# Keys' products moved behind each attention chunk's outputs, with a filled prologue and later weight splits

## The chip, the core and the metric

One NeuronCore of one Trainium2 chip runs the whole program. The metric is the time of one execution on the device, in microseconds (us), from the first to the last instruction with what lies around them; lower is better. TensorE (PE in the rows) multiplies matrices into PSUM banks, VectorE (DVE), ScalarE (ACT) and GpSimd (POOL) work on tiles, SyncE (SP) issues the DMA transfers. Each engine runs its own list of instructions in order, and they wait for one another through semaphores.

## What is computed

A "macaron" block on 4 x 1024 tokens of 128 features: half a gated ternary FFN, a linear attention block with its own small FFN, and half a ternary FFN again (cut to what matters):

```
x = x + 0.5 * ternary_ffn(layernorm(x))
x = x + attention_block(layernorm(x))
x = x + 0.5 * ternary_ffn(layernorm(x))

# ternary_ffn: silu(x@w1*s1) * (x@w2*s2), gelu(h@h1*s), gelu(h@h2*s), h@w3*s
# attention_block:
x = x + linear_attention(ln(x));  x = x + gelu(ln(x) @ Wf1) @ Wf2
# linear_attention, 16 heads of 64, phi = elu + 1:
Q = phi(x @ Wq); K = phi(x @ Wk); V = x @ Wv
S = cumsum(K^T V); z = cumsum(K)           # over tokens
out = (Q S) / max(Q z, 1e-6) @ Wo
```

Products run in a two-part form: each fp32 operand is split into a rounded "high" part and the rest, its "low" part, and two or three matmuls replace one.

## The kernel before

The program has four stages, which follow one another: the first ternary FFN (to about 190 us), the attention (to about 590 us), its small FFN (to about 625 us), the second ternary FFN (to the end). In the ternary FFNs tokens run in tiles of 512, two tiles ("A" and "B") at a time, four pairs per FFN.

**Attention** works in 32 chunks of 128 tokens; two chunks, even `e` and odd `o`, make one pass of `pair(hh)`, and passes 1 to 14 are one loop on TensorE. For chunk `g` TensorE does, in this order: `state_products(g)` (`D`, 64 matmuls of 64 rows by 64 columns, the chunk's K^T V by halves), `scores(g)` (`S`, 64 small ones), the keys' product of the next chunk (`K`, `token_major("K", ...)`: 6 matmuls of 128x512), and `outputs(g)`: first `I`, 64 small matmuls of the queries with the state so far, then `O`, 64 small ones that add the masked scores times the values. After that come the norm's transposes and values (behind an even chunk: also the output projection of the pair before), or the queries and values (behind an odd one), the transposes of keys (`KT`) and of outputs (`OT`), and the next `D`.

VectorE serves each chunk from its own list: `accumulated(g)` adds D's banks to the running state (`sm`, tile `middle`; then `ss`, tile `state`; two halves each), `masked(g)` multiplies the two banks of scores by the mask (`am`), `low_outputs(g)` makes the low parts of the outputs of the chunk before (`ol`), `divided(g)` divides O's banks by the denominator (`ot`), and `phi` finishes keys and queries from ScalarE's exp and relu.

D, I and O write the same four PSUM banks (`OB`, banks 2 to 5). So `outputs(g)` begins with a wait until VectorE has read D's banks, which is the last `ss`; and between I and O stands a wait for the last `am`:

```
emptied([f"O{g}.{j}{m}" for j in range(2) for m in "ab"])        # L962: ahead of I
hold(*([made(X["dve"], f"am{g}b")] if j == 0 else []), ...)      # L976: ahead of O
```

The four other banks (0, 1, 6, 7: `RING`) go round among all 512-column products; `turn()` takes the next one, and a product waits until the reader of the bank's tenant before has done.

**The prologue.** TensorE starts with the transposes of the first two normalised tiles, waits for the first weight split (`weight(0)`: high and low part of piece 0) and does the first products with three matmuls each, until a flag shows that two will do. VectorE makes the high and low parts of the six weight pieces (`high(k)`, `low(k)`: tiles `wh`, `wl`) and, in the first FFN's passes, those of the attention's and the small FFN's weights (`staged(k)`: tiles `fh`, `fl`, `wah`, `wal`, from the transfer into `stage` that SyncE issues). The second tiles' statistics and normalisation (`xn`) come behind `low(1)`, `low(2)`, `high(5)`. In the taken branch TensorE waits for high parts only: pieces 1 and 2 ahead of the hidden layer H1, pieces 3, 4 and 5 ahead of H2. GpSimd makes the low parts of all hidden activations (`al`, L1895).

**The end.** The last two tiles' results are transposed into the same bank 7, so B's transposes wait until VectorE has added A's (`back`, `dve_res`).

Of the kernel before, what the change touches and what calls it, by code (L numbers as in the profile page):

```python
# [5 lines left out]
P = 128  # L6
# [106 lines left out]
def build_kernel(nc, t, out):  # L113
# [37 lines left out]
    with ctx:  # L151
# [223 lines left out]
        def attention_plan():  # L375
# [49 lines left out]
            def transposed(banks, g):  # L425
                for j in range(2):
                    job(banks[j], f"OT{g}.{j}", "dve", f"ol{g}.{j}")
                    act.append(f"oh{g}.{j}")
                    dve.append(f"ol{g}.{j}")
# [25 lines left out]
            for hh in range(NHALF):  # L455
                e, o, last = 2 * hh, 2 * hh + 1, hh + 1 == NHALF
                pairs.append({"pe": len(pe), "act": len(act), "dve": len(dve), "pool": len(pool)})

                for h in range(2):
                    phi(turn(), f"K{o}.{h}")  # L460
                outputs(e)
# [16 lines left out]
                if hh:  # L478
                    job(bank, f"yT{hh - 1}", "dve", f"y{hh - 1}")
                    dve.append(f"y{hh - 1}")  # L480
                transposed((turn(), turn()), e)
                if last:
                    tail(turn(), "N1", "dve_fn", "lo", 1)
                state_products(o, (turn(), turn()))

                if last:
# [8 lines left out]
                    transposed((2, 5), o)  # L495
                    for m in range(2, 4):
# [17 lines left out]
                turn()  # L514
                transposed((turn(), turn()), o)
                state_products(o + 1, (turn(), turn()))
            X = phase(1, pe=pe, act=act, dve=dve, pool=pool)
# [41 lines left out]
        def _(sp):  # L559
# [7 lines left out]
            def tern_dma(f):  # L567
# [8 lines left out]
                for i in range(NI):  # L576
# [4 lines left out]
                    if n == 0:  # L581

                        wait(sp, "dve_wa", "lo", i)
                        sp.dma_start(stage[:, :], t["attn"][i]).then_inc(in_a, 16)
# [5 lines left out]
                    elif n == 0 and i == NI - 2:  # L590

                        wait(sp, "dve_xnA", "xn", off + i + 1)
                        sp.dma_start(ax[:, :, :], view(x1_d)[0]).then_inc(in_ax, 16)
                    for u, U in enumerate(PAIR):
# [85 lines left out]
        def _(pe):  # L680
# [13 lines left out]
            def tern_pe(f, terms, start=None, end=None, head=None):  # L694
# [10 lines left out]
                def back(u, U, n):  # L705

                    wait(pe, f"act_y{U}", "y", n)
                    wait(pe, f"dve_res{before(U, n)[0]}", "res", before(U, n)[1])
                    transposes(ps[7], [yf[u][:, q * P:(q + 1) * P] for q in range(Q)], T[f"pe_y{U}"], "T")

                def product(job, col, hi_in, lo_in, terms, ready=None):
# [14 lines left out]
                def first(u, U, n, terms, ms=range(KT)):  # L726
# [3 lines left out]
                    for m in ms:  # L730
                        for x, w in (("g", W1), ("v", W2)):
                            product(("L1", U, m, x, n), lambda k: w + m * P, hi_in, lo_in, terms)
# [11 lines left out]
                if head:  # L744
                    weight(0)
                    first(0, "A", off, terms, range(KT - 1))
# [286 lines left out]
            def pair(hh):  # L1033
                e, o = 2 * hh, 2 * hh + 1
                for h in range(2):
                    token_major("K", o, h)
                outputs(e)
# [11 lines left out]

                for h in range(2):  # L1050
                    token_major("K", o + 1, h)
                outputs(o)
# [9 lines left out]
            def last_pair(hh):  # L1062
                e, o = 2 * hh, 2 * hh + 1
                for h in range(2):
                    token_major("K", o, h)
                outputs(e)
# [346 lines left out]
        def _(dve):  # L1413
# [37 lines left out]
            def tern_dve(f, start=None):  # L1451
# [46 lines left out]
                def residual(u, U, n):  # L1498
# [4 lines left out]
                    added(u, ps[7][:, :]).then_inc(*T[f"dve_res{U}"].step("res"))  # L1503
# [6 lines left out]
                if nf == 0:  # L1510
# [33 lines left out]
                    low(1)  # L1544
                    low(2)
                    high(5)
# [6 lines left out]
                for n in range(off, off + NI):  # L1553
                    more, i = n + 1 < off + NI, n - off
                    if more:
                        for u, U in enumerate(PAIR):
                            stats(u, U, n + 1)
                        for u, U in enumerate(PAIR):
                            normalise(u, U, n + 1)
                    elif start:  # L1560
                        start()
                    if nf == 0:

                        if n == 0:
                            for k in (3, 4, 5):
                                low(k)
# [493 lines left out]
```

## Time and profile before

| | |
|---|---|
| Median of 3 runs | 819.98 us (818.83 to 820.84) |
| The profiled execution | 821.32 us |
| its span, first to last instruction | 819.6 us |
| TensorE busy | 790.0 us, 96% of the span |
| VectorE, ScalarE, GpSimd busy | 71%, 68%, 43% |
| mean granted TensorE clock | 0.999 |

In the rows further down a timeline row gives the start in us from the span's start, the duration (of a merged group: from its first start to its last end), engine and line, the operation, what it writes and reads, its size and how many were merged; in square brackets stands how long the engine sat idle ahead of it and what ended that. Matmuls overlap, so two rows' starts tell more than their durations: the difference of starts is what a group takes on the engine.

### The profile page before, as it was taken

Reading aid. Unit: us, or ns where it says so; the run is one execution under the profiler, and the core shown is the slowest. Engines: PE = TensorE matmul, PEld = TensorE weight load, DVE = VectorE, ACT = ScalarE, POOL = GpSimd, SP = SyncE. Lnnn points to the kernel's source line nnn. Section 1 sums busy time; section 2 is a strip of 40 time slices with the busy share of each in tenths; the row PEclk is TensorE's granted clock in tenths of the full one; section 3 lists DMA queues with packets and bytes.
Section 4 is the critical chain, followed back from the end, with each engine's and each line's share of the span. In section 5 each row is a group of like instructions: output and inputs, shape, how many; then the busy total and the mean of one; then the engine's idle time right before and its main releaser. Section 6 shows DMA issues by size and latency. Waiting matters only on the chain.

```text
span 819.6 us, 27796 instructions
## 1 busy us (share of the span) xinstructions
PE 790.0 (96%) x11690; PEld 671.7 (82%) x11690; DVE 578.6 (71%) x1332; ACT 558.1 (68%) x1005; POOL 353.0 (43%) x281
## 2 busy tenths in 40 slices
PE   4999999999999999999999999999999999999997
PEld 3777878887788888898888898888888788888885
DVE  7977665556878798787797878889789673728210
ACT  4677887778555666656665656665688787877774
POOL 2897989782001001010100101000155697979784
PEclk9999999999999999999999999999999999999999
DMA  7013020201001001010010101102024320201010
GB/s 244 1 41 88 26 77 14 70 9 53 16 3 40 13 0 52 0 52 0 1 51 0 52 0 39 51 0 56 24 79 116 91 65 14 65 13 40 10 43 28
DMA packets 56700, 33.53 MB, mean 41 GB/s; under 512 B 1984, under 2 KB 55232, under 8 KB 56640
## 3 DMA queue, kind: packets, MB, share of 16 engines
q1 hardware_dynamic: 56640, 32.79, 13.8%
q8 instruction: 31, 0.51, 0.3%
q14 instruction: 29, 0.24, 0.1%
HBM read 22.29 MB, written 10.49 MB: 40 GB/s over the span
## 4 chain that ended last, share of the span: by engine, by line
PE 81%; ACT 8%; POOL 3%; issue 3%; DVE 3%; ACTq 0%; DVEq 0%
PE ps L722 34%; PE ps L908 17%; PE ps L684 9%; PE ps L802 5%; PE ps L971 4%; PE ps L998 4%; PE ps L982 4%; PE ps L954 4%; ACT ee L1307 3%; ACT rr L1308 3%; POOL alA L1895 1%; ACT vt L1329 1%; POOL alB L1895 1%; ACT gate L1165 0%; DVE full L1475 0%
## 5 line engine op out<-in xcount | busy, mean ns | idle before, releaser
L1307 ACT ACTIVATE ee<-ps 128x512 f32<-128x512 f32 x128 | 78.4, 613 | 101.1 <-PE ps L908 98.7
L1895 POOL TENSOR_TENSOR alA<-full,ahA 128x512 fp32r<-128x512 f32 x82 | 111.1, 1368 | 57.0 <-DVE ahA L1483 25.6
L1988 POOL TENSOR_TENSOR as<-as,power 128x4 f32<-128x4 f32 x16 | 19.0, 1188 | 270.6 <-DVE as L1690 239.4
L1895 POOL TENSOR_TENSOR alB<-full,ahB 128x512 fp32r<-128x512 f32 x84 | 112.0, 1345 | 22.8 <-ACT ahB L1186 7.7
L1475 DVE SCALAR_TENSOR_TENSOR full<-ps,sc,gate 128x512 f32<-128x512 f32 x64 | 46.6, 747 | 97.1 <-PE ps L722 60.1
L722 PE MATMUL ps<-ahA,wh 128*128 128x512 f32 x288 | 113.3, 394 | 0.0
L722 PE MATMUL ps<-ahB,wh 128*128 128x512 f32 x288 | 113.3, 393 | 0.0
L722 PE MATMUL ps<-alA,wh 128*128 128x512 f32 x288 | 112.2, 390 | 0.0
L722 PE MATMUL ps<-alB,wh 128*128 128x512 f32 x288 | 112.2, 390 | 0.0
L1185 ACT ACTIVATE full<-ps,sc 128x512 f32<-128x512 f32 x86 | 59.5, 692 | 33.7 <-PE ps L722 19.7
L1308 ACT ACTIVATE rr<-ps 128x512 f32<-128x512 f32 x128 | 79.1, 618 | 0.0
L722 PEld LDWEIGHTS ps<-alA,wh 128*128 128x128 f32 x288 | 54.1, 188 | 10.9
L722 PEld LDWEIGHTS ps<-ahA,wh 128*128 128x128 f32 x288 | 54.1, 188 | 10.9
L722 PEld LDWEIGHTS ps<-alB,wh 128*128 128x128 f32 x288 | 54.1, 188 | 10.9
L722 PEld LDWEIGHTS ps<-ahB,wh 128*128 128x128 f32 x288 | 54.1, 188 | 10.9
L908 PE MATMUL ps<-wah,ahh 128*128 128x512 f32 x128 | 55.0, 430 | 1.1 <-DVE ol L1772 0.5
L1772 DVE TENSOR_TENSOR ol<-ps,oh 128x512 fp32r<-128x512 f32 x64 | 41.2, 686 | 15.8 <-ACT oh L1349 15.8
L908 PE MATMUL ps<-wah,ahl 128*128 128x512 f32 x128 | 50.3, 393 | 0.7 <-issue 0.7
L908 PE MATMUL ps<-wal,ahh 128*128 128x512 f32 x128 | 50.3, 393 | 0.0
L1670 DVE SCALAR_TENSOR_TENSOR qf<-ee,rr 128x512 f32<-128x512 f32 x64 | 43.0, 687 | 6.1 <-ACT rr L1308 6.0
L1670 DVE SCALAR_TENSOR_TENSOR kt<-ee,rr 128x512 f32<-128x512 f32 x64 | 42.6, 689 | 6.6 <-ACT rr L1308 6.5
L1744 DVE TENSOR_TENSOR ot<-ps,rden 128x512 f32<-128x512 f32 x64 | 44.3, 692 | 2.4 <-DVE rden L1740 0.2
(189 smaller groups left out, 2178.1 us busy)
## 6 DMA issues: line engine op xcount, KB each, us to landing
wst<-in_ternary SPq DMA_DIRECT2D x5, 512.0 KB, 7.7
stage<-in_attn SPq DMA_DIRECT2D x4, 512.0 KB, 4.2
xlnA<-x_scratch SPq DMA_DIRECT2D x8, 256.0 KB, 2.8
axr<-x_scratch SPq DMA_DIRECT2D x8, 256.0 KB, 3.1
yx_scratch<-ay SPq DMA_DIRECT2D x8, 256.0 KB, 2.3
xs_scratch<-axs SPq DMA_DIRECT2D x8, 256.0 KB, 2.4
xlnA<-yx_scratch SPq DMA_DIRECT2D x8, 256.0 KB, 2.8
xlnB<-yx_scratch SPq DMA_DIRECT2D x8, 256.0 KB, 3.0
```

The costliest lines, as they stand in the source:

```text
L684: ins = nc.tensor.transpose(dst[:, k * P:(k + 1) * P], src, ident[:, :])
L722: ins = nc.tensor.matmul(b[:, :], w[:, col(k):col(k) + P], x_[:, k, :], start=(k == 0 and j == 0), stop=(k == ks[-1] and j == terms - 1))
L802: ins = nc.tensor.matmul(b[:, :], w, x_, start=(n == 0), stop=(n == len(parts) - 1))
L908: ins = nc.tensor.matmul(b, w, m, start=(n == 0), stop=(n == len(parts) - 1))
L1185: nc.scalar.activation(fullh[k % NH][:, :], src, ACT.Gelu, scale=s_).then_inc(*T[f"act_{h}{U}"].step(f"full{m}"))
L1307: nc.scalar.activation(ee[k][:, :], src[:, :], ACT.Exp).then_inc(*X["act"].step(f"e_{name}"))
L1308: nc.scalar.activation(rr[k][:, :], src[:, :], ACT.Relu).then_inc(*X["act"].step(f"r_{name}"))
L1475: nc.vector.scalar_tensor_tensor(fulll[m][:, :], ps[f["bank"]["L1", U, m, "v", n]][:, :], sc[:, KT + m:KT + m + 1], gate[k % NS][:, :], AL ...
L1670: nc.vector.scalar_tensor_tensor(dst, e_, 1.0, r_, ALU.min, ALU.add)\
L1744: nc.vector.tensor_tensor(dst, src[:, :, :, 0:DH], rden[:, j, :, :].unsqueeze(3).to_broadcast([P, 2, HP, DH]), ALU.mult)\
L1772: nc.vector.tensor_tensor(ol[:, 4 * j:4 * j + 4, own], ps[X["banks"].bank[f"OT{g}.{j}"]][:, :].rearrange("p (k n) -> p k n", n=P), oh[:, 4 ...
L1895: return nc.gpsimd.tensor_tensor(dst, src, hi.bitcast(F32), ALU.subtract)
```

## The change

Four edits, which don't touch what is computed.

1. **Attention, TensorE.** In every pass `outputs(e)` and `outputs(o)` stand ahead of the next chunk's keys' product, so K comes behind O instead of between S and I. The turn of the bank ring that was skipped ahead of `transposed(o)` is now skipped at the top of the pass.
2. **Attention, VectorE.** `divided` stands ahead of the keys' `phi`, and `low_outputs` behind `accumulated` and `masked` (in the last pass only behind the odd chunk; there `low_outputs(e)` stays ahead).
3. **Prologue and first FFN.** TensorE does 21, 2 and 6 transposes of the identity whose results nobody reads, ahead of, between and behind the first two tiles' transposes. The first product's third matmul alone waits for the low part of piece 0. `low(1)`, `low(2)`, `high(5)` move behind the normalisation of the second A tile, `staged(0)` (`fh`, `fl`) out of the first pass's middle to its end, the others one place later; SyncE issues the transfer into `stage` behind the loads of `xln`.
4. **The end.** The last tile B is transposed into bank 6 and no longer waits for A's addition.

```
@@ attention_plan / pair, on TensorE
+                outputs(e)
+                turn()
                 for h in range(2):
                     phi(turn(), f"K{o}.{h}")
-                outputs(e)
...
+                outputs(o)
                 for h in range(2):
                     phi(turn(), f"K{o + 1}.{h}")
-                outputs(o)
...
                 kt((OB[0] + 1, turn()), o + 1)
-                turn()
                 transposed((turn(), turn()), o)
                 state_products(o + 1, (turn(), turn()))
+                low_parts(o)
@@ attention_dve
-                    for j in range(2):
-                        low_outputs(e, j)
                     accumulated(o)
...
                     masked(o)
+                    if not last:
+                        for j in range(2):
+                            low_outputs(e, j)
...
+                    accumulated(o + 1)
+                    masked(o + 1)
                     for j in range(2):
                         low_outputs(o, j)
-                    accumulated(o + 1)
-                    masked(o + 1)
@@ prologue, on TensorE
+            def unread(count):
+                for _ in range(count):
+                    nc.tensor.transpose(ps[5][:, 0:P], ident[:, :], ident[:, :])
+
             all_before(pe, weights)
-            for u, U in enumerate(PAIR):
+            for (u, U), count in zip(enumerate(PAIR), (21, 2)):
+                unread(count)
                 tern_norm(u, U, 0)
+            unread(6)
...
                         for j, (x_, w) in enumerate(((hi_in, wh), (lo_in, wh), (hi_in, wl))[:terms]):
+                            if third and j == 2:
+                                pe.wait_ge(*third)
@@ tern_dve
-                        for u, U in enumerate(PAIR):
-                            normalise(u, U, n + 1)
+                        normalise(0, "A", n + 1)
+                        if (nf, i) == (0, 0):
+                            low(1)
+                            low(2)
+                            high(5)
+                        normalise(1, "B", n + 1)
...
                         wait(dve, "act_H2A", "hi1", n)
-                        staged(i if i == 0 else i + 1)
+                        staged((1, 3, 4)[i - 1])
...
-                    if nf == 0 and n == 0:
-                        dve.wait_ge(*weights["act"].done("flag", 0))
-                        staged(1)
+                    if nf == 0 and i < 2:
+                        if i == 0:
+                            dve.wait_ge(*weights["act"].done("flag", 0))
+                        staged((0, 2)[i])
@@ the end
+        def back_ps(U, n):
+            return ps[6 if (U, n) == ("B", 2 * NI - 1) else 7]
```

TensorE's list, from D of chunk 0 to the norm's transposes, before (`ps<-vt,kt` is D, `ps<-qf,kf` S, `wah,ahh` K and V, `state,qf` and `middle,qf` I, `vt,am` O, `ident,axn` the norm's transposes):

```order
L998 MATMUL ps<-vt,kt 64x65 x32
L954 MATMUL ps<-qf,kf 64x64 x32
L908 MATMUL ps<-wah,ahh 128x512
L908 MATMUL ps<-wah,ahl 128x512
L908 MATMUL ps<-wal,ahh 128x512
...
L971 MATMUL ps<-state,qf 64x65 x2
L971 MATMUL ps<-middle,qf 64x65 x2
...
L982 MATMUL ps<-vt,am 64x65 x32
L684 MATMUL ps<-ident,axn 128x128 x2
```

and of the change, same place:

```order
L1013 MATMUL ps<-vt,kt 64x65 x32
L969 MATMUL ps<-qf,kf 64x64 x32
L986 MATMUL ps<-state,qf 64x65 x2
L986 MATMUL ps<-middle,qf 64x65 x2
...
L997 MATMUL ps<-vt,am 64x65 x32
L923 MATMUL ps<-wah,ahh 128x512
L923 MATMUL ps<-wah,ahl 128x512
L923 MATMUL ps<-wal,ahh 128x512
...
L695 MATMUL ps<-ident,axn 128x128 x2
```

The six matmuls of K have moved from between S and I to behind O; nothing stands between S and I any more.

VectorE's list at the end of a pass, before (from the next norm `axn` to the denominators of the next chunk):

```order
L1715 TENSOR_SCALAR axn<-xoB,as 128x128 x2
L1772 TENSOR_TENSOR ol<-ps,oh 128x4x128 x2
L1761 TENSOR_TENSOR middle<-ps,state 128x260 x2
L1761 TENSOR_TENSOR state<-ps,middle 128x260 x2
L1732 TENSOR_TENSOR am<-ps,mask 128x512 x2
L1670 SCALAR_TENSOR_TENSOR kt<-ee,rr 128x8x64 x2
L1739 TENSOR_SCALAR den<-ps 128x8
```

and of the change:

```order
L1739 TENSOR_SCALAR axn<-xoB,as 128x128 x2
L1785 TENSOR_TENSOR middle<-ps,state 128x260 x2
L1785 TENSOR_TENSOR state<-ps,middle 128x260 x2
L1756 TENSOR_TENSOR am<-ps,mask 128x512 x2
L1796 TENSOR_TENSOR ol<-ps,oh 128x4x128 x2
L1763 TENSOR_SCALAR den<-ps 128x8
```

The two `ol` have moved behind the two `am`, and the keys' `kt` behind the divisions.

## Rows read from the trace of the kernel before

**Rows 1.** The page's first line; one pass by windows: PE, PEld, DVE, ACT, POOL

```profile
span 819.6 us, 27796 instructions
...
340.00:364.73 24.73, 24.46 (x633) 21.84 (x628) 20.48 (x57) 15.09 (x31) 2.92 (x3) 1.00 0.11 32
```

**Rows 2.** Timeline of TensorE, behind an odd chunk: D, S, K, I, O, queries

```profile
359.81 1.16 PE L998 MATMUL ps<-vt,kt 64*64 64x65 f32 x64
360.80 1.12 PE L954 MATMUL ps<-qf,kf 64*64 64x64 f32 x64
361.84 0.50 PE L908 MATMUL ps<-wah,ahh 128*128 128x512 f32 x1
...
363.40 0.28 PE L971 MATMUL ps<-state,qf 64*64 64x65 f32 x2
...
364.39 1.12 PE L982 MATMUL ps<-vt,am 64*64 64x65 f32 x64
365.44 0.38 PE L908 MATMUL ps<-ahh,wah 128*128 128x256 f32 x1
```

**Rows 3.** Timeline of VectorE, the same chunk

```profile
360.10 1.29 DVE L1772 TENSOR_TENSOR ol<-ps,oh 128x512 fp32r<-128x512 f32 x2 [0.63 <-ACT oh L1349]
361.31 0.75 DVE L1761 TENSOR_TENSOR middle<-ps,state 128x260 f32<-128x260 f32 x2
...
362.65 1.28 DVE L1732 TENSOR_TENSOR am<-ps,mask 128x512 f32<-128x512 f32 x2
```

**Rows 4.** Timelines of TensorE (D) and VectorE, chunk 0, which has no `ol`

```profile
197.68 1.16 PE L998 MATMUL ps<-vt,kt 64*64 64x65 f32 x64 [0.47 <-ACT vt L1329]
...
198.51 0.82 DVE L1761 TENSOR_TENSOR middle<-ps,state 128x260 f32<-128x260 f32 x2 [1.14 <-PE ps L998]
199.25 0.75 DVE L1761 TENSOR_TENSOR state<-ps,middle 128x260 f32<-128x260 f32 x2
199.92 1.28 DVE L1732 TENSOR_TENSOR am<-ps,mask 128x512 f32<-128x512 f32 x2
```

**Rows 5.** Timeline of TensorE, an even chunk: transposes of outputs, D, norm's transposes

```profile
346.35 1.15 PE L684 MATMUL ps<-ident,ot 128*128 128x128 f32 x8 [0.24 <-ACT vt L1329]
347.43 1.16 PE L998 MATMUL ps<-vt,kt 64*64 64x65 f32 x64
...
353.20 0.44 PE L684 MATMUL ps<-ident,axn 128*128 128x128 f32 x2
```

**Rows 6.** Timeline of TensorE, the prologue

```profile
8.77 1.09 PE L684 MATMUL ps<-ident,xnA 128*128 128x128 f32 x4 [8.77 <-DVE xnA L1443]
...
12.49 0.77 PE L722 MATMUL ps<-nhA,wh 128*128 128x512 f32 x1 [1.44 <-DVE wl L1523]
...
18.83 0.39 PE L722 MATMUL ps<-nhA,wh 128*128 128x512 f32 x1
19.06 0.39 PE L722 MATMUL ps<-nlA,wh 128*128 128x512 f32 x1
```

**Rows 7.** Timelines of TensorE, VectorE and GpSimd, first pass of the first FFN

```profile
41.43 0.66 PE L684 MATMUL ps<-ident,xnA 128*128 128x128 f32 x4 [0.89 <-DVE xnA L1443]
...
63.31 0.50 PE L722 MATMUL ps<-nhA,wh 128*128 128x512 f32 x1 [1.35 <-ACT yfA L1192]
...
28.36 3.59 DVE L1523 TENSOR_TENSOR wl<-wst,wh 128x1024 fp32r<-128x1024 f32 x2
31.87 1.52 DVE L1518 CAST wh<-wst 128x512 fp32r<-128x512 f32 x1
...
37.07 4.31 DVE L1443 SCALAR_TENSOR_TENSOR xnA<-xlnA,bagA,rsA 128x128 f32<-128x128 f32 x4
...
25.78 7.32 POOL L1895 TENSOR_TENSOR alB<-full,ahB 128x512 fp32r<-128x512 f32 x4 [0.46 <-DVE ahB L1483]
...
44.52 2.65 POOL L1895 TENSOR_TENSOR alB<-full,ahB 128x512 fp32r<-128x512 f32 x2
```

**Rows 8.** Timeline of TensorE, the last tile's transposes

```profile
814.26 0.63 PE L684 MATMUL ps<-ident,yfB 128*128 128x128 f32 x4 [0.88 <-DVE xoA L1449]
```

More of the change, by code:

```diff
@@ L428, in transposed, with low_parts @@
                     act.append(f"oh{g}.{j}")
-                    dve.append(f"ol{g}.{j}")
+            def low_parts(g):
+                dve.extend(f"ol{g}.{j}" for j in range(2))
             def state_products(n, banks):
@@ L478, in attention_plan @@
                 if hh:
-                    job(bank, f"yT{hh - 1}", "dve", f"y{hh - 1}")
+                    job(OB[0] + 1 if last else bank, f"yT{hh - 1}", "dve", f"y{hh - 1}")
                     dve.append(f"y{hh - 1}")
@@ L483, in attention_plan @@
                     tail(turn(), "N1", "dve_fn", "lo", 1)
+                if last:
+                    low_parts(e)
                 state_products(o, (turn(), turn()))
+                if not last:
+                    low_parts(e)
                 if last:
@@ L593, in tern_dma @@
                         sp.dma_start(ax[:, :, :], view(x1_d)[0]).then_inc(in_ax, 16)
+                    if n == 0:
+                        wait(sp, "dve_wa", "lo", i)
+                        sp.dma_start(stage[:, :], t["attn"][i]).then_inc(in_a, 16)
                     for u, U in enumerate(PAIR):
@@ L707, in back, with product @@
                     wait(pe, f"act_y{U}", "y", n)
-                    wait(pe, f"dve_res{before(U, n)[0]}", "res", before(U, n)[1])
-                    transposes(ps[7], [yf[u][:, q * P:(q + 1) * P] for q in range(Q)], T[f"pe_y{U}"], "T")
-                def product(job, col, hi_in, lo_in, terms, ready=None):
+                    if back_ps(U, n) is ps[7]:
+                        wait(pe, f"dve_res{before(U, n)[0]}", "res", before(U, n)[1])
+                    transposes(back_ps(U, n), [yf[u][:, q * P:(q + 1) * P] for q in range(Q)], T[f"pe_y{U}"], "T")
+                def product(job, col, hi_in, lo_in, terms, ready=None, third=None):
                     name, U, m, x, n = job
@@ L724, in product, with first @@
                     ins.then_inc(*T[f"pe_{name}{U}"].step("y" if name == "W3" else f"{x}{m}"))
-                def first(u, U, n, terms, ms=range(KT)):
+                def first(u, U, n, terms, ms=range(KT), third=None):
                     hi_in, lo_in = (a[u][:, :].rearrange("p (k n) -> p k n", k=1) for a in (nh, nl))
@@ L744, in tern_pe @@
                 if head:
-                    weight(0)
-                    first(0, "A", off, terms, range(KT - 1))
+                    pe.wait_ge(*weights["dve"].done("hi0", 0))
+                    first(0, "A", off, terms, range(KT - 1), weights["dve"].done("lo0", 0))
                     head()
@@ L1034, in pair @@
                 e, o = 2 * hh, 2 * hh + 1
+                outputs(e)
                 for h in range(2):
                     token_major("K", o, h)
-                outputs(e)
                 norm(hh + 1)
@@ L1048, in pair @@
                 scores(o)
+                outputs(o)
                 for h in range(2):
                     token_major("K", o + 1, h)
-                outputs(o)
                 for j in range(4):
@@ L1063, in last_pair @@
                 e, o = 2 * hh, 2 * hh + 1
+                outputs(e)
                 for h in range(2):
                     token_major("K", o, h)
-                outputs(e)
                 for h in range(2):
@@ L1820, in attention_dve @@
                         residual(hh - 1)
-                    if hh + 2 == NHALF:
-                        after("dve", f"y{hh - 1}")
-                        f_normalise(0)
-                    for j in range(2):
-                        low_outputs(e, j)
+                    if last:
+                        for j in range(2):
+                            low_outputs(e, j)
                     accumulated(o)
@@ L1829, in attention_dve @@
                     masked(o)
+                    if not last:
+                        for j in range(2):
+                            low_outputs(e, j)
                     if c == 0 and i + 1 < NT:
                         once(i + 1)
+                    elif hh + 2 == NHALF:
+                        after("dve", f"y{hh - 1}")
+                        f_normalise(0)
                     if last:
@@ L1842, in attention_dve @@
                         continue
+                    for j in range(2):
+                        divided(o, j)
                     for h in range(2):
                         phi(f"K{o + 1}.{h}")
-                    for j in range(2):
-                        divided(o, j)
                     for j in range(4):
```

22 lines of the change are left out of this document (9 added, 13 removed).

## The prediction, made before the changed kernel ran

> **What bounds the kernel now.** I read the busy shares first, then TensorE's timeline through one pass of the attention, then VectorE's beside it, and last the few places where TensorE waits. TensorE is the bound: in one attention pass it is busy 24.46 of 24.73 us, VectorE 20.48, ScalarE 15.09 [rows 1]. So only what TensorE waits for, or what it takes for a group, moves the end. The reader should see two things in the chunk of [rows 2, 3]. First, TensorE goes from D to S to K to I to O without a gap, and from the start of D to the start of the queries it takes 365.44 - 359.81 = 5.63 us. Second, VectorE is late beside it and nobody minds: `middle` and `state` run from 361.31, `am` until 362.65 + 1.28 = 363.93, and O, which needs `am`, starts at 364.39. K, 363.40 - 361.84 = 1.56 us of TensorE work that needs nothing from VectorE's state, is what covers this chain. The change takes that cover away and moves `ol` (1.29 us for the two) out of the chain's way in exchange.
>
> **Attention, the term that decides.** How long is the chain when no `ol` stands in it? Chunk 0 shows it [rows 4]: D starts at 197.68; `middle` starts 0.83 us later, since it must wait for D's first half; the last `state` ends at 200.00, D + 2.32; the last `am` at 201.20, D + 3.52. VectorE was idle for 1.14 us ahead of it, so this is the chain at its shortest, and moving `ol` can't make it shorter. In the changed kernel the wait ahead of I is for the last `state` and the wait ahead of O for the last `am`. A release costs little: `xnA` ends at 37.07 + 4.31 = 41.38 and the transposes that wait for it start at 41.43, 0.05 us [rows 7]; I take 0.10 here, because weights of small tiles have to be loaded first. So, counted from the start of D:
> - TensorE could start I at 2.03 at the latest (361.84 - 359.81, where K started), but starts it at 2.32 + 0.10 = 2.42.
> - I takes 0.99 (364.39 - 363.40), so it is through at 3.41; O may start at 3.52 + 0.10 = 3.62.
> - O takes 1.05 (365.44 - 364.39): 4.67.
> - K behind O: six matmuls at 0.23 each (19.06 - 18.83, [rows 6]) are 1.38; between small tiles it took 1.56. I take 1.42: 6.09.
>
> Behind an odd chunk this is 6.09 against 5.63, a loss of 0.46 us. Behind an even one, 353.20 - 347.43 = 5.77 before [rows 5]; but there K's first bank is the one whose reader is the second `ol`. With `ol` behind `am` that reader ends at about 3.52 + 1.2 = 4.7, is seen at 4.8, and K waits 0.13; K is also followed by another kind of product (0.05). 6.27 against 5.77: 0.50. There are 31 chunks with a K behind them, 15 odd and 16 even: 15 x 0.46 + 16 x 0.50 = 14.9 us. Moving `divided` ahead of `phi` costs nothing while the keys' transposes come over 3 us behind K. One cost more: ScalarE now gets the keys' and queries' exp back to back, and TensorE already waits 0.24 us for its copies ahead of the transposes of outputs [rows 5]. That wait grows by 0 to 0.1 us in 15 passes; I take 0.05, 0.7 us. **Attention: +15.6 us.** Ends: with a release of 0.05, K at 1.38 and no wait for `ol`, 6.00 in every chunk, 15 x 0.37 + 16 x 0.23 = 9.2 us; with 0.65 everywhere (a later release by 0.15), 20 us.
>
> On K's place a rule stands beside the row. The rows give K 1.56 us between S and I, and six matmuls of 1.38 us at the steady rate, so 0.18 us of a chunk is the change between 64 and 128 wide work. The Trainium skill, "TensorEngine Tiling (Array Packing)", Key Properties, says that changing the tiling mode drains TensorE; it speaks for the move, the trace agrees that a change costs something, and it puts no figure on it.
>
> **Prologue.** TensorE is idle until 8.77 and waits 1.44 us for the low part of piece 0; from 12.49 to 18.83 it does 15 matmuls in 6.34 us, 0.42 each, and 0.23 from then on [rows 6]: the lower of its two clock levels, 1.2 GHz, then 2.4 GHz after some 6 us of unbroken work. The added transposes fill the time from the start, so the higher level should come by about the first product. At most 15 x (0.42 - 0.23) = 2.8 us and the first two matmuls' 1.1 us of earlier start come free, 3.9 together. VectorE has its splits and sums to do in between whatever TensorE's rate, so I take -2.5 (0 to -3.9).
>
> **Second A and B tile.** `low(1)`, `low(2)` (3.59 us) and `high(5)` (1.52) no longer stand ahead of `xnA` [rows 7], so TensorE's wait of 0.89 us for it goes. What is late next is `high(5)`, which TensorE needs right behind those transposes: it stands behind `xnA` now. `xnA` itself still waits for GpSimd, which finishes its four `al` first, so it moves earlier than 41.38 by 2.5 to 7.6 us and `high(5)` ends 5.1 us behind it, between 38.9 and 44.0; TensorE is there at about 41.4 - 0.9 - 2.5 + 0.7 = 38.7. It waits 0.2 to 5.3 us. I take 1.2, near the early end, since GpSimd is relieved too: net +0.3.
>
> **Later splits.** At 63.31 TensorE waits 1.35 us for ScalarE, and with the waits around it about 2.5 us in that stretch; ScalarE is late there because it waits for GpSimd's low parts. GpSimd's four `al` that lie beside VectorE's two `wl` take 7.32 / 4 = 1.83 us each, two others 2.65 / 2 = 1.33 [rows 7]. With `fh` and `fl` (some 4 us of such work) gone from the pass's middle and the `wl` spread, GpSimd gains some 2 us or more. I take -2.3 (0 to -2.5). The Trainium skill, "GPSIMD Engine Reference", Specifications, says that GpSimd shares its SBUF interfaces with VectorE and that they contend when VectorE has two SBUF inputs; it names the cause of the 1.83, and by it the added `wah` split at the end of the second pass would cost GpSimd again, where TensorE has no wait now. The moved transfers of SyncE keep several us to spare. **First FFN: -2.5 + 0.3 - 2.3 = -4.5 us** (ends +1 and -8).
>
> **The end.** TensorE is idle 0.88 us ahead of the last transposes, for VectorE's addition [rows 8]; the row doesn't show how soon ScalarE's own result lets the transposes start, so I take half: -0.45 us (0 to -0.88).
>
> **Sum.** +15.6 - 4.5 - 0.45 = +10.65. The profiled execution took 821.32 us, 1.34 above the median 819.98 (span 819.6, [rows 1]): 832.0 for such an execution, 830.6 as a median.
>
> **Rivals.**
> - *TensorE is not held by the chain (faster).* If I and O start behind S at once, each chunk saves the change of width: K gives back 1.56 and the 0.15 us of switching ahead of it, and costs 1.42 behind O, so about -0.25 to -0.3 x 31 = -8 to -9 us, and with the rest 806 to 807. It decides if the last `am` comes before D + 3.0, the time at which D, S and I are through. For it: the kernel before never waits there. Against: 3.52 with VectorE idle ahead [rows 4]. 0.07.
> - *The chain is partly covered*: a quick release, K at the steady rate, no wait for `ol`: 820.0 + 9.2 - 4.5 - 0.45 = 824. 0.13.
> - *The first FFN gives nothing*: the clock comes no earlier or `high(5)` eats it: 820.0 + 15.6 - 0.45 = 835. 0.16.
> - *Both partly*, the chain short and every gain of the first FFN taken: 820.0 + 9.2 - 8 - 0.9 = 820.3, within 0.3%. 0.04.
> - My forecast, 0.60.
>
> **How the numbers follow.** A measurement of this kernel can tell some 0.3%, 2.5 us, from no change. Faster by more: 0.07 (the first rival). Within: 0.04. Slower by more: the forecast and the two rivals at 824 and 835, 0.89. The range from 822 to 838 leaves out the first and fourth rival and the far ends of the unknown costs (841 at most).
>
> **What would show it.** In the profile of the changed kernel: TensorE idle ahead of the first I matmul by some 0.4 us with VectorE's `state` as releaser, and ahead of O by 0.2 with `am`, in every chunk; a pass of about 25.7 us instead of 24.73; `middle` starting 0.75 to 0.85 us behind D; a first product at 0.23 us a matmul; no wait for `xnA` near 40, but one for `wh`. The forecast is wrong if I follows S without a gap, if `am` ends earlier than D + 3.4, or if the first FFN saves more than 8 us.

## The result, and the profile after

| | before | changed |
|---|---|---|
| median, same chip | 820.12 us (4 runs) | 837.18 us (835.91 to 838.3, 4 runs) |
| ratio | | 1.0209, 95% interval 1.019 to 1.0229 |
| profiled execution | 821.32 us | 836.85 us |
| its span | 819.6 us | 834.8 us |
| TensorE busy | 790.0 us | 801.5 us |

The change costs 17 us. The forecast was 830.6 us with a range of 822 to 838: the sign and the mechanism came out as forecast, the size 6.6 us higher. The ratios leave out two slow executions, one of the kernel before (4389.25 us) and one of the prologue alone (1156.21 us; without it that kernel's median is 816.4 instead of the 816.74 given below).

First the page's line and one attention pass of the changed kernel by windows, from D of chunk 12 to D of chunk 14 (width, then busy time of PE, PEld, DVE, ACT, POOL, the granted clock, the DMA share and GB/s). It answers to [rows 1]: the pass takes 26.06 us instead of 24.73, and TensorE is busy in 25.09 of them, so it idles for about 1 us of a pass instead of 0.3.

```profile
span 834.8 us, 27782 instructions
...
350.98:377.04 26.06, 25.09 (x621) 22.10 (x621) 21.62 (x61) 14.89 (x31) 3.33 (x3) 1.00 0.14 41
```

TensorE's timeline through the odd chunk 13, which answers to [rows 2]:

```profile
363.96 1.16 PE L1013 MATMUL ps<-vt,kt 64*64 64x65 f32 x64
364.94 1.12 PE L969 MATMUL ps<-qf,kf 64*64 64x64 f32 x64
366.43 0.27 PE L986 MATMUL ps<-state,qf 64*64 64x65 f32 x2 [0.38 <-DVE state L1785]
...
367.58 1.16 PE L997 MATMUL ps<-vt,am 64*64 64x65 f32 x64
368.68 0.50 PE L923 MATMUL ps<-wah,ahh 128*128 128x512 f32 x1
369.01 0.40 PE L923 MATMUL ps<-wah,ahl 128*128 128x512 f32 x1
...
370.17 0.28 PE L923 MATMUL ps<-ahh,wah 128*128 128x256 f32 x1
```

and VectorE's, which answers to [rows 3, 4]:

```profile
364.72 0.90 DVE L1785 TENSOR_TENSOR middle<-ps,state 128x260 f32<-128x260 f32 x2 [1.10 <-PE ps L1013]
365.53 0.75 DVE L1785 TENSOR_TENSOR state<-ps,middle 128x260 f32<-128x260 f32 x2
366.20 1.28 DVE L1756 TENSOR_TENSOR am<-ps,mask 128x512 f32<-128x512 f32 x2
367.40 1.28 DVE L1796 TENSOR_TENSOR ol<-ps,oh 128x512 fp32r<-128x512 f32 x2
```

The reader should lay the two on top of each other. The last `state` ends at 366.28 and I starts at 366.43; the last `am` ends at 367.48 and O starts at 367.58. VectorE had been idle for 1.10 us ahead of `middle`, so it works as early as D lets it, and TensorE now waits for it twice. In the kernel before, I started 1.34 us after the last `state` had ended, and O 0.46 us after the last `am` [rows 2, 3]. The list of TensorE's waits (us in total, times, longest) of the changed kernel has the wait ahead of I in its first line; the one ahead of O, some 0.1 us, shows only by the starts:

```profile
PE ps L986 <- DVE state L1785: 10.1, 27, 0.6
...
PE ps L817 <- DVE nlA L1627: 1.5, 1, 1.5
PE ps L736 <- DVE wh L1540: 1.4, 1, 1.4
PE ps L695 <- ACT vt L1351: 1.3, 1, 1.3
```

Where the 15.2 us between the two spans lie, by the starts of D on TensorE's timeline:

| stretch | before | changed | difference |
|---|---|---|---|
| start to D of chunk 0 | 197.68 | 193.39 | -4.3 |
| chunks 0 to 3 | 50.72 | 53.52 | +2.8 |
| chunks 4 to 28 (25 chunks) | 309.29 | 324.85 | +15.6, 0.62 each |
| chunks 29 and 30 | 28.34 | 27.78 | -0.6 |
| D of chunk 31 to the end | 233.57 | 235.21 | +1.6 |

### The profile page after: what moved, and what is told of

Read it like the earlier page. It is cut to its first block, busy times and chain, and to the rows that moved or that the text cites. A ratio compares the mean times of both kernels' runs of the same rounds, so it can differ in the third digit from the quotient of the medians.

```text
span 834.8 us, 27782 instructions
## 1 busy us (share of the span) xinstructions
PE 801.5 (96%) x11719; PEld 679.1 (81%) x11719; DVE 578.8 (69%) x1332; ACT 553.5 (66%) x1005; POOL 347.7 (42%) x281
## 4 chain that ended last, share of the span: by engine, by line
PE 71%; DVE 14%; ACT 8%; issue 6%; POOL 1%; DMA 0%; SPq 0%; DVEq 0%; ACTq 0%; POOLq 0%
PE ps L736 36%; PE ps L923 11%; PE ps L695 8%; PE ps L817 5%; PE ps L1013 4%; ACT rr L1330 4%; ACT ee L1329 3%; PE ps L997 3%; PE ps L986 3%; DVE am L1756 2%; DVE state L1785 2%; DVE ol L1796 2%; DVE ot L1768 1%; DVE qf L1694 1%; POOL alB L1923 1%
## 5 line engine op out<-in xcount | busy, mean ns | idle before, releaser
L2016 POOL TENSOR_TENSOR as<-as,power 128x4 f32<-128x4 f32 x16 | 16.4, 1023 | 286.7 <-DVE as L1714 249.4
L1497 DVE SCALAR_TENSOR_TENSOR full<-ps,sc,gate 128x512 f32<-128x512 f32 x64 | 46.6, 747 | 97.7 <-PE ps L736 68.6
L923 PE MATMUL ps<-wah,ahh 128*128 128x512 f32 x128 | 56.7, 443 | 0.6
L986 PE MATMUL ps<-state,qf 64*64 64x65 f32 x1024 | 37.0, 220 | 11.2 <-DVE state L1785 10.1
L1785 DVE TENSOR_TENSOR middle<-ps,state 128x260 f32<-128x260 f32 x64 | 27.3, 428 | 27.7 <-PE ps L1013 26.6
```

The source lines that it names most:

```text
L923: ins = nc.tensor.matmul(b, w, m, start=(n == 0), stop=(n == len(parts) - 1))
L986: ins = nc.tensor.matmul(banks[j][m][tok, place[p]], qf[rows, p, first:first + DH], (middle if half else state[k])[rows, p, :], start=(p = ...
L1497: nc.vector.scalar_tensor_tensor(fulll[m][:, :], ps[f["bank"]["L1", U, m, "v", n]][:, :], sc[:, KT + m:KT + m + 1], gate[k % NS][:, :], AL ...
L1785: ins = nc.vector.tensor_tensor(after_[:, pairs, :], src, before_[:, pairs, :], ALU.add)
```

## The experiments

All numbers are medians, with the kernel before run on the same chip (821.1, 821.1, 820.0 and 821.1 us in the four comparisons). "Rest" is short for edits 3 and 4.

**1. Rest alone** (attention as in the kernel before).

> Edits 3 and 4 alone: attention in the order of the kernel before, prologue, splits and the end as changed. By the stages of the two traces the first FFN starts attention 4.3 us earlier and the end gives 0.5 to 0.7, so 815.2 us. The rival: the 3 us that the changed kernel lost between the last regular attention chunk and the last FFN come from the earlier arrival, not from the attention's order; then 818.

Measured: 814.16 us, ratio 0.992 (0.9904 to 0.9937). The same program once more, in another comparison:

> The same program as in the run of edits 3 and 4 alone, on the chip of this comparison: 814.2 us. If the stalls inside small matmuls in the first four attention chunks belong to where the code lies, D of chunk 0 to D of chunk 4 takes 47.8 us again, within 0.3; if they are chance, anything from 47.5 to 50.7.

813.5 us, ratio 0.9923 (0.9906 to 0.9939). So edits 3 and 4 make the kernel faster by 6.5 to 6.9 us, and without the attention's edits there is a version that beats both. Of this 4.4 us lie ahead of D of chunk 0 (193.33), as forecast for the first FFN, and 0.45 behind D of chunk 31, as forecast for the end. One part was in no term of the forecast: 2.9 us come in chunks 0 to 3, 47.84 us instead of 50.72. TensorE stalls there inside runs of 64 small matmuls, for no reason that the profile names. In the kernel before, in chunk 1:

```profile
209.17 0.80 PE L954 MATMUL ps<-qf,kf 64*64 64x64 f32 x41
211.30 0.57 PE L954 MATMUL ps<-qf,kf 64*64 64x64 f32 x23 [1.33 <-issue]
```

Such stalls stand in code that runs for the first time (chunks 0 to 3, and again the last pass), not in chunks 4 to 28. The repeated program gave 48.29 us for the four chunks, 0.45 more than at first and so a little outside the expected 0.3, with the same single stall of this kind, 0.57 us in chunk 3; other programs with the same attention code gave 49.35, 50.17 and 50.72. So they belong to the program more than to chance. What they come from was not shown.

**2. The attention's edits alone** (edits 1 and 2).

> Edits 1 and 2 alone. If the stages add up: 820.1 + 17.6 (30 chunks) + 3.1 (last pair and small FFN) = 841 us, and the chunks are as long as in the changed kernel, 12.95 us from D to D. Rival as above: 838.

Measured: 841.55 us, ratio 1.0254 (1.0236 to 1.0271), 20.5 us more than before. Chunks 4 to 28 take 324.58 us, 12.98 each, as in the changed kernel. Chunks 0 to 3 take 54.94, 4.2 more than before. D of chunk 31 to the end takes 235.23, 1.7 more, with the wait for `nlA` of the small FFN at the same place as in the changed kernel; the rival, that this comes from an earlier arrival, is out. The two parts add up to 20.5 - 6.7 = 13.8, and together they cost 17.1. Of these 3.3 us, 1.5 lie in the stalls of chunks 0 to 3 (-2.9 and +4.2 apart, +2.8 together), 0.9 in the first FFN, where this kernel reached D at 196.81 with the same code as before, which needed 197.68, and 0.4 behind D of chunk 31.

**3. K behind the outputs, VectorE's list as before** (edit 1 and rest).

```
 outputs(e); K          # TensorE as changed
 phi(K); divided(e); ... low_outputs(e); accumulated(o); masked(o)    # VectorE as before
```

> The changed kernel with VectorE's list in attention as before (ol ahead of sm, phi ahead of the divisions), K behind O. If VectorE's chain D, sm, ss, am sets I and O, then ol (1.2 us) stands in it again: I starts at about D + 3.1, O at D + 4.2, 0.6 us later than in the changed kernel; 837 + 31 x 0.4 = 849 to 856 us, more where the outputs' transposes wait for divisions. Rival, the place of K costs by itself: 837.

Measured: 871.29 us, ratio 1.0614 (1.0596 to 1.0632). I starts at D + 3.06 and O at D + 4.21 in the odd chunks, as computed. The even ones are later still (3.63 and 4.78), and TensorE gets a second wait, ahead of the outputs' transposes, for ScalarE's relu of the last query:

```profile
416.04 1.14 PE L693 MATMUL ps<-ident,ot 128*128 128x128 f32 x8 [0.72 <-ACT rr L1328]
```

The chain's length sets I and O in the odd chunks, as expected. The total of 849 to 856 us was 15 us too low: what the even ones and the second wait add, 0.6 us and 0.7, was not in the expectation.

**4. VectorE's new order alone** (edit 2 and rest).

```
 K; outputs(e)          # TensorE as before
 divided(e); phi(K); ... accumulated(o); masked(o); low_outputs(e)    # VectorE as changed
```

> Edit 2 with edits 3 and 4, K left between S and I. If only VectorE's chain mattered this would be 814 us as edits 3 and 4 alone, since K covers the chain. But K's two banks are those of the outputs' transposes, which ol reads, and ol now ends behind am: K's first matmul would start at D + 4.2 instead of D + 2.03, about 2.15 us a chunk, 31 x 2.15 = 67 us: 881 us.

Measured: 904.79 us, ratio 1.1025 (1.099 to 1.1059). Here the K that follows D of chunk 11, which starts at 359.99:

```profile
364.17 0.50 PE L929 MATMUL ps<-wah,ahh 128*128 128x512 f32 x1 [2.08 <-DVE ol L1802]
```

K starts at D + 4.18, as computed. So `ol` behind `am` can't be had with K where it was and the ring as it is: the ring's four banks hold two tenants that `ol` reads and two that `am` reads, and K needs two of them. In the changed kernel the same `ol` costs next to nothing: it ends at D + 4.71, and K starts at D + 4.77 in the even chunks, 0.05 later than in the odd ones. The 24 us beyond the expectation are told in the section on the hardware.

**5. A short chain.** In the changed kernel `sm`, `ss` and `am` on 16 columns:

```
-tensor_tensor(after_[:, pairs, :], src, before_[:, pairs, :], ALU.add)
+tensor_tensor(after_[:, pairs, 0:16], src[:, :, 0:16], before_[:, pairs, 0:16], ALU.add)
...and am[:, m, :, 0:16] likewise
```

> The changed kernel with sm, ss and am on 16 of their 64 or 65 columns (three quarters of the state's sum and of the masked scores are left out), so the chain from D to the last am is over 1 us shorter; everything else stays. If the chain is what holds I and O, both waits go (0.45 and 0.1 us in each of 31 chunks) and the time is 837 - 18 = 819 us or less. Rival, K behind O costs by its place, its bank and ScalarE: 837, unchanged.

Measured: 822.71 us, ratio 1.002 (1.0009 to 1.0031): 14.5 us less than the changed kernel (15.5 by the two ratios). TensorE in its odd chunk 13:

```profile
360.32 1.16 PE L1013 MATMUL ps<-vt,kt 64*64 64x65 f32 x64
361.30 1.12 PE L969 MATMUL ps<-qf,kf 64*64 64x64 f32 x64
362.25 0.28 PE L986 MATMUL ps<-state,qf 64*64 64x65 f32 x2
...
363.20 1.14 PE L997 MATMUL ps<-vt,am 64*64 64x65 f32 x64
364.27 0.50 PE L923 MATMUL ps<-wah,ahh 128*128 128x512 f32 x1
...
365.75 0.28 PE L923 MATMUL ps<-ahh,wah 128*128 128x256 f32 x1
```

Both waits are gone, and chunks 4 to 28 take 309.48 us, within 0.2 of rest alone (309.51) and of the kernel before (309.29). That is the case of the first rival, made real, and it shows two things. The whole 0.62 us a chunk goes with the chain: K behind O costs nothing on balance by its place, its bank or ScalarE. (`ol` stands behind the chain and ends 0.9 us earlier here too, so what K waits for its bank, 0.05 us at most, isn't told apart.) And the 0.25 to 0.3 us that the rival promised for one change of width less are not there either: the odd chunks gain 0.17 (12.21 us instead of 12.38), the even ones lose 0.16 (12.54). In the even ones two costs stand against the gain: the pass now begins with I, which starts 0.37 us behind the last of S where the loop turns, against 0.11 in the odd chunks, and the first two matmuls of the output projection take 0.18 us more than in rest alone. Its span is still 8.0 us above that of rest alone (820.1 against 812.1), all outside the steady chunks: 5.3 in chunks 0 to 3, 2.6 behind D of chunk 31, 2.1 ahead of D of chunk 0 (three memsets on VectorE, which fill once what is no longer written), less 2.0 in chunks 29 and 30.

**6. Only the state's part of the chain short** (`am` whole).

> The changed kernel with only sm and ss on 16 of 65 columns (three quarters of the state's sum are left out), am whole. I no longer waits: it starts at about D + 2.05 instead of D + 2.47. If the chain to the last am sets O, O follows the masks, which now start as soon as S is through: D + 2.13 + 1.28 + 0.1 = 3.5 instead of 3.62, so the 0.4 us gained ahead of I is lost again ahead of O: 31 x 0.12 = -4, 833 us. Rival, the wait ahead of I is the loss: 31 x 0.4 = -12 to -13, 824 us.

Measured: 836.73 us, ratio 1.0203 (1.0186 to 1.022), the changed kernel's time within its spread. TensorE in the odd chunk 13, where D starts at 365.39:

```profile
367.32 0.28 PE L986 MATMUL ps<-state,qf 64*64 64x65 f32 x2
...
368.91 1.16 PE L997 MATMUL ps<-vt,am 64*64 64x65 f32 x64 [0.43 <-PE ps L986]
```

I starts at D + 1.93 instead of 2.47 and O at D + 3.52 instead of 3.62: 0.1 us a chunk (322.49 us for 25 chunks instead of 324.85, 2.4 in all) is left of the 0.54 gained ahead of I, and the three memsets ahead of chunk 0, where D comes at 195.22 instead of 193.39, take 1.8 of these 2.4. The row names I as the releaser, but I was long through; the masks end at 368.81:

```profile
367.52 1.29 DVE L1756 TENSOR_TENSOR am<-ps,mask 128x512 f32<-128x512 f32 x2 [0.35 <-PE ps L969]
```

The idle time of 0.35 us ahead of them is new: they now wait for S itself. The first of two waits on one chain is not its price.

**7. The prologue alone, the splits alone.**

> The kernel before with only the unread transposes and the third-matmul wait of edit 3. The prediction's term: -2.5 us up to the hidden layer's first matmul; if the later stalls near 40 and 63 us keep their places, most of it is given back by VectorE's and GpSimd's lists and the first FFN ends 0 to 2.5 us earlier. The 2.9 us that edits 3 and 4 gained in the first four attention chunks lie in stalls inside runs of small matmuls; if they depend on where the code lies (the 29 added transposes shift TensorE's list), they appear here too: 816 to 818. If they come from the moved splits: 818 to 820.

> The kernel before with only the moved splits and transfers of edit 3. The prediction's term: +0.3 - 2.3 = -2.0 us in the first FFN. First four attention chunks: 50.7 us as before if their stalls depend on where TensorE's code lies (819), 47.9 if the splits made them (816).

Measured: prologue 816.74 us, ratio 0.9944 (0.9927 to 0.9961); splits 817.99, ratio 0.9967 (0.9954 to 0.998). D of chunk 0 comes at 195.19 with the one and 195.37 with the other, against 197.68 before and 193.33 with both: -2.5 and -2.3 us, and they nearly add up, to 4.4. The waits of TensorE up to D of chunk 0, with the prologue alone:

```profile
PE ps L724 <- ACT yfA L1202: 1.4, 1, 1.4
PE ps L684 <- DVE xnA L1453: 0.9, 1, 0.9
...
PE ps L724 <- ACT ahB L1196: 0.5, 1, 0.5
```

and with the splits alone:

```profile
PE ps L722 <- DVE wl L1523: 1.4, 1, 1.4
PE ps L722 <- DVE wh L1518: 1.4, 1, 1.4
```

The moved splits take away the waits for `xnA`, `yfA` and `ahB` and put one of 1.4 us for `high(5)` in their place. Nothing of the prologue's 2.5 us is given back at 40 or 63 us. The cause that the forecast named for the later splits shows as well: between 36 and 66 us ScalarE waited 9.0 us for GpSimd's low parts in the kernel before, and with the splits alone no such wait is left in the list. The first four attention chunks take 49.35 and 50.17 us, neither the 47.84 of both nor clearly one cause: the stalls there follow neither the added transposes nor the splits alone.

**8. Three tries to go below rest alone.** In rest alone TensorE still waits 0.24 us for ScalarE's `vt` ahead of the outputs' transposes in each odd chunk, 0.40 more than between two groups of transposes without a wait [rows 5]; and it idles for 1.41 us ahead of the product that needs `high(5)`. `high(5)` is moved in all three. First another turn of the ring, with `high(5)` ahead of `low(1)` and `low(2)`:

```
+turn()                                  # ahead of the next values
 values(turn(), o + 1, h)
 kt((OB[0] + 1, turn()), o + 1)
-turn()
```

> Edits 3 and 4 with attention in the old order, and two moves more. The skipped turn of the bank ring stands ahead of the odd chunk's next values instead of ahead of the outputs' transposes, so their first bank is one that ScalarE emptied long ago: the wait of 0.40 us in each of 15 passes should shrink to 0.05, -5 us. high(5) stands ahead of low(1) and low(2): the wait of 1.58 us ahead of H1 goes, -1.5 us if nothing is late next. 814.2 - 6.5 = 807.7. Rival: ScalarE's copy of vt, which D needs as well, takes the wait over: 813.

Measured: 814.98 us, ratio 0.9933 (0.9915 to 0.9951). `high(5)` gave what was expected, D of chunk 0 at 191.91 instead of 193.33. The ring gave nothing: the rival was right in kind, but the wait went to the values' products, since their banks' tenants are now the last queries, which ScalarE reads late. Chunks 4 to 28 take 310.58 us, 1.1 more. Second, values into the outputs' own banks:

```
 divided(o); phi(K)                      # VectorE, odd chunk
-values(turn(), o + 1, h)
+values(OB[1] + h, o + 1, h)    # and no turn is skipped any more
```

> Edits 3 and 4 with attention in the old order, high(5) ahead of low(1) and low(2), and the odd chunk's values written into the second pair of output banks (4 and 5), which VectorE's divisions empty (these stand ahead of the keys' phi in the odd chunk) and whose next tenant, D, waits for ScalarE's copy of the values already. The ring then needs no skipped turn, and neither the values nor the outputs' transposes wait for a bank that ScalarE still reads. Expected: the 0.40 us ahead of the outputs' transposes goes in 15 passes, -6 us; 814.2 - 6 - 0 to 1.4 = 807 to 808. Rival: D waits for vt instead, 813 to 814.

Measured: 815.55 us, ratio 0.9951 (0.9934 to 0.9967). The transposes wait no more, but D does, and chunks 4 to 28 take 311.00 us:

```profile
339.29 0.92 PE L1008 MATMUL ps<-vt,kt 64*64 64x65 f32 x47 [0.35 <-ACT vt L1346]
```

Both say the same: the banks only choose who waits; ScalarE is late with `vt` at the end of its twelve passes over keys and queries, behind an idle time of 1.5 us. The third try fills that idle time, with one query product ahead of I (and a fourth pair of buffers for exp and relu):

```
 K
+queries(hh + 1, 0)
 outputs(o)
-queries(hh + 1, 0..3)
+queries(hh + 1, 1..3)
```

> Edits 3 and 4 with attention in the old order, high(5) ahead of low(1) and low(2), the first of the four query products of an odd chunk ahead of I (behind K), and a fourth pair of buffers for exp and relu. ScalarE idles 1.5 us between the keys' and the queries' exp and is then 0.4 us late with the copy of the values; with Q.0 ahead of I its queue should be through 0.5 us earlier, so neither the outputs' transposes nor D wait: 15 x 0.40 = -6 us, and -1.4 us from high(5): 813.8 - 7.4 = 806.5. A chunk pair of 24.35 us instead of 24.73. Rival: Q.0's bank is the first scores' bank, whose mask product ends at about D + 3.5; if that is late, Q.0 waits and the gain is eaten: 813.

Measured: 811.08 us (810.79 to 811.41), ratio 0.9881 (0.9864 to 0.9897), the fastest of all: 10 us below the kernel before and 26 below the changed one. TensorE's rows, D of chunk 13 at 349.20:

```profile
352.77 0.39 PE L918 MATMUL ps<-ahh,wah 128*128 128x256 f32 x1
353.00 0.28 PE L918 MATMUL ps<-ahh,wal 128*128 128x256 f32 x1
...
359.35 1.03 PE L690 MATMUL ps<-ident,kt 128*128 128x128 f32 x8
360.36 1.15 PE L690 MATMUL ps<-ident,ot 128*128 128x128 f32 x8
361.44 0.29 PE L1008 MATMUL ps<-vt,kt 64*64 64x65 f32 x4
```

The transposes of outputs follow those of keys by 1.01 us instead of 1.27 (of these 0.87 are the eight transposes themselves), so 0.26 of the 0.40 us are gone, but 0.12 come back where the query product was put in: it starts 0.28 us behind K's last matmul, and its own first takes 0.23 us instead of 0.12. An odd chunk gains 0.14 us, not 0.40. The expectation had the mechanism and three times the size, and its rival was there in small: the query product starts 0.05 us behind the first mask product, which ends at D + 3.52. Of the 3.1 us by which this span lies below that of rest alone, 1.5 are `high(5)`'s (D of chunk 0 at 191.85), 1.8 come in chunks 4 to 28, 1.3 in chunks 0 to 3 (46.55 us), where the stalls without a cause lie, and behind chunk 28 it loses 1.5.

## Why the forecast was right, and where it was not

By its own steps, against the two spans: forecast +10.65 us, measured +15.2. The median of 837.18 lies only 0.8 us inside the top of the range, and one of the four executions, 838.3, outside. The attention as a whole cost 19.9 us (2.8 + 15.6 - 0.6, and 2.1 behind D of chunk 31, see below) where the forecast had 15.6 and 20 as its far end; measured alone, edits 1 and 2 cost 20.5. That the time fell inside the range owed something to luck: the 1.6 us by which chunks 29 and 30 came out below the forecast, for no reason that it had named.

*TensorE bounds, and K covers VectorE's chain.* Right, shown by the short chain: without the chain's length the steady chunks take what they took before.

*The chain's length from chunk 0* [rows 4]. Right to the hundredth where it mattered: O at D + 3.62, as forecast; I at D + 2.47, forecast 2.42. The release took 0.15 us ahead of I and 0.10 ahead of O, forecast 0.10 for both. `middle` started 0.76 us behind D, inside the 0.75 to 0.85 that the forecast had set as a sign.

*K behind O.* This term was too small. From O to K 1.10 us instead of 1.05, and K itself 1.49 instead of 1.42: its first matmul holds the engine for 0.33 us wherever K stands (369.01 - 368.68), which the forecast had taken for a cost of its old place. The even chunk gives this sum, from D to the norm's transposes, 6.26 us against a forecast of 6.27:

```profile
350.98 1.16 PE L1013 MATMUL ps<-vt,kt 64*64 64x65 f32 x64
...
357.24 0.38 PE L695 MATMUL ps<-ident,axn 128*128 128x128 f32 x2
```

The odd chunk came to 6.21 us instead of 6.09, a loss of 0.58 instead of 0.46. In the even chunk another 0.12 us are lost further on: the first two matmuls of the output projection take 0.18 us more, and the norm's transposes give 0.05 back. The same 0.18 stands in the kernel with the short chain, so it isn't the chain's; what ends it was not separated.

*ScalarE.* The forecast let its wait ahead of the outputs' transposes grow by 0.05 us in each odd chunk. The size is near, the place is not. That wait is gone: the transposes of outputs follow those of keys by 1.16 us instead of 1.27. Another came, which costs 0.19 us on average between the queries and the transposes of keys: the second product of the next values takes the bank of the second query, and ScalarE's relu reads it late.

```profile
373.37 0.59 ACT L1330 ACTIVATE rr<-ps 128x512 f32<-128x512 f32 x1
...
374.01 0.50 PE L923 MATMUL ps<-wah,ahh 128*128 128x512 f32 x1
```

The relu ends at 373.96, and the product starts 0.49 us behind the matmul before it instead of 0.23. Net of the two, ScalarE costs 0.08 us in an odd chunk.

Together a steady chunk loses 0.62 us, with the forecast at 0.48 and 0.02 more for ScalarE: +3.0 us over 25 chunks, the largest part of the miss.

*The ends of the attention.* The forecast took all 31 chunks as alike. Chunks 0 to 3 lost 0.8 us more than four steady ones would by the forecast, of which a wait of 1.3 us for ScalarE's `vt` in chunk 0 is one that shows. Chunks 29 and 30 lost nothing but gained 0.6: chunk 29 took 13.61 us before, with a wait of 0.5 for the second `ol` ahead of K, and takes 12.89 now. That is 1.6 us less than forecast. Behind D of chunk 31 the forecast had nothing for the attention, and the stretch came out 2.1 us above it. One part shows: before, TensorE waited 1.60 us for `nlA` in chunk 30; now a wait for it stands in the small FFN, and the changed order has other waits in chunk 30 in its place. First before, then changed:

```profile
584.39 0.41 PE L684 MATMUL ps<-ident,ayf 128*128 128x128 f32 x2 [1.60 <-DVE nlA L1603]
```

```profile
598.50 0.63 PE L695 MATMUL ps<-ident,ot 128*128 128x128 f32 x4 [0.73 <-ACT kf L1361]
...
613.69 0.50 PE L817 MATMUL ps<-ahA,fh 128*128 128x512 f32 x1 [1.54 <-DVE nlA L1627]
```

The forecast never looked at the last pass. Here is where a step was missing and not only mis-sized.

*Prologue*: -2.5 forecast, -2.5 measured alone. The granted clock rose to its higher level at 9.2 us instead of 18.6, and from the second product on the matmuls come 0.23 us apart, where before they came 0.42 apart until 18.6 [rows 6]. The first product starts at 10.91 instead of 12.49 and waits 0.34 us ahead of its third matmul, for the low part of piece 0. The second one's first two:

```profile
12.29 0.39 PE L736 MATMUL ps<-nhA,wh 128*128 128x512 f32 x1
12.52 0.40 PE L736 MATMUL ps<-nlA,wh 128*128 128x512 f32 x1
```

*Second A and B tile*: the wait for `xnA` went and one for `high(5)` came, as forecast, 1.42 us where 1.2 were taken [rows 7]:

```profile
37.92 0.60 PE L695 MATMUL ps<-ident,xnA 128*128 128x128 f32 x4
39.94 0.47 PE L736 MATMUL ps<-ahA,wh 128*128 128x512 f32 x1 [1.42 <-DVE wh L1540]
```

*Later splits*: with the term before, -2.0 forecast and -2.3 measured alone. One reading under it was too coarse: 1.83 us is the mean of four `al`, of which the first two take 1.30 and 1.53 us and only the last two, which lie fully beside VectorE's splits, 2.27 and 2.28. So GpSimd loses about 0.95 us on each of those two against the 1.33 of an undisturbed one, and next to nothing on the others. *First FFN in all*: -4.5 forecast, -4.3 measured.

*The end*: -0.45 forecast. The last transposes wait 0.34 us for ScalarE instead of 0.88 for VectorE [rows 8], a gain of 0.5:

```profile
830.17 0.66 PE L695 MATMUL ps<-ident,yfB 128*128 128x128 f32 x4 [0.34 <-ACT yfB L1214]
```

*The rivals.* That TensorE isn't held is out; when the chain was shortened so that it was true, it gave 822.7 and not 806, so this rival was wrong by its price too, in the change of width and at the attention's ends. That the chain is partly covered (824) and that the first FFN gives nothing (835) are both out by the stages, and so is the rival at 820.3, which took the short chain and more from the first FFN; that the time lies near 835 is chance. The other 2 us, between the 15.2 of the spans and the 17.1 of the medians, come mostly from the profiled execution of the kernel before, 1.2 us above its median, and that of the changed one, 0.3 below.

## What to carry to other kernels

A product that needs nothing and stands between a producer and its consumer may be what pays for another engine's chain: before moving it, add up that chain from a place where it runs with nothing ahead of it, from the instruction that starts it to the last release. Two waits that hang on one chain are one cost, and shortening the link that the profile names only moves the wait to the next. And a loop's steady turn, however exactly it is summed, says nothing of the first and last pass: there this forecast was off by 0.8, 1.6 and 2.1 us, in both directions.

## What the runs showed of the hardware

**The granted clock fell, again and again, in the kernel with the longest waits.** With VectorE's new order alone, TensorE waits some 2.1 us in each chunk. By windows in chunk 12 of that kernel (columns as in the windows above; the granted clock is the figure behind POOL):

```profile
376.09:379.50 3.41, 1.33 (x66) 1.15 (x58) 3.37 (x8) 0.00 (x0) 0.00 (x0) 1.00 0.00 0
379.50:382.91 3.41, 3.41 (x54) 2.48 (x56) 1.45 (x11) 2.17 (x4) 1.01 (x1) 0.50 0.00 0
382.91:386.00 3.09, 3.09 (x101) 2.76 (x94) 1.97 (x7) 1.30 (x3) 0.00 (x0) 1.00 0.00 0
```

TensorE had waited 2.08 us shortly ahead of the fall, and then ran for 3.41 us at the lower of its levels, 1.2 GHz, with matmuls of 512 columns 0.43 us apart instead of 0.23, before 2.4 GHz came back. It happened in 16 chunks, not in all, though nearly each had a wait of about this length (62.3 us in 30 times); an even chunk with it took 15.93 us and one without 14.40. 16 x 1.5 = 24 us, about the distance of 904.8 from the expected 881. In the third experiment, with 1.5 us of waiting ahead of I in the even chunks and 0.95 in the odd ones, the clock fell once in the attention, behind a wait of 2.53 us.

**Where the width of the work changes**, the first matmul of 128 rows starts 0.15 us behind the last of 64 (368.68 against 368.53 in the changed kernel, the same behind S in the kernel before); from I to O, both of 64 rows, it was 0.04 in the kernel before. The Trainium skill, "TensorEngine Tiling (Array Packing)", Key Properties, says that changing the mode drains TensorE, and these rows agree. But halving the number of such changes, as in the short chain, left the steady chunks at 309.5 us: in this kernel the changes saved bought nothing on balance.

**Stalls without a named cause** of up to 1.3 us stand inside the first runs of small matmuls, and sum to several us: the first four attention chunks took between 46.6 and 50.7 us in kernels whose attention keeps K between S and I and VectorE's list as before. Differences of 3 us between two programs can lie in this alone.
